# One square root fewer in the softmax reciprocal of an attention and expert-layer kernel

## The reference

```
h = layernorm(x)
q, k, v = split(h @ Wqkv.T)            # 16 heads of 64 features
lam = sigmoid(relu(log(t+1) @ Wl1.T) @ Wl2.T)   # one number per head and position
# attention inside 8 chunks of 256 positions
s = (q_chunk . k_chunk) / 8 * lam[key]
x = x + (softmax(s) @ v_chunk) @ Wout.T + bout
h = layernorm(x)
# 8 experts of width 1408, the two best per position, weighted by the softmax of the gate
# and a shared expert of width 2816, weighted by a sigmoid
x = x + sum_e w_e * down_e(silu(gate_e(h)) * up_e(h)) + sigmoid(h . seg) * shared(h)
```

## Time and profile before

| | |
|---|---|
| median of 3 runs | 3646.75 us (3646.26 to 3648.06) |
| the profiled execution | 3649.09 us, its slowest core's span 3647.6 us |
| spans of the 8 cores in it | 3639.4 to 3647.6 us, granted clock 0.894 to 0.897 |
| TensorE busy | 2927.1 us, 80% |
| VectorE busy | 1252.2 us, 34% |
| ScalarE busy | 906.0 us, 25% |

### The profile page before, as it was taken

The page is one execution under the profiler, slowest core; times in us unless marked ns, Lnnn a source line. Parts: engine busy times, 40 slices in busy tenths (PEclk is TensorE's granted clock), DMA queues, the critical chain, the costliest instruction groups (busy, mean ns, idle before and its releaser), DMA issues.

```text
span 3647.6 us, 38537 instructions; the slowest of 8 cores (3639.4 to 3647.6 us)
## 1 busy us (share of the span) xinstructions
PE 2927.1 (80%) x13760; PEld 1369.7 (38%) x13988; DVE 1252.2 (34%) x2411; ACT 906.0 (25%) x1560; POOL 58.0 (2%) x70
## 2 busy tenths in 40 slices
PE   0446545545645599999999999999999999999998
PEld 0223313313313244444444444444444444444443
DVE  0323323322322333333333333333333333334333
ACT  0275465465466211111111111111111111110110
POOL 0100000000000000000000000000000000000000
PEclk9966667757757699999999999999999999999999
DMA  8100000000000413203232032212320223203203
GB/s 163 23 1 1 1 1 1 1 1 1 1 1 1 69 27 52 44 3 50 44 52 39 6 52 44 37 23 37 53 44 9 44 44 52 44 1 53 44 1 93
DMA packets 14029, 114.31 MB, mean 31 GB/s; under 512 B 1931, under 2 KB 2060, under 8 KB 8212
## 3 DMA queue, kind: packets, MB, share of 16 engines
q0 software_dynamic: 6832, 94.95, 15.7%
q1 hardware_dynamic: 7012, 16.89, 1.8%
HBM read 198.39 MB, written 8.39 MB: 57 GB/s over the span
## 4 chain that ended last, share of the span: by engine, by line
PE 74%; ACT 11%; DVE 6%; issue 5%; SPq 2%; ACTq 1%; DVEq 0%; DMA 0%; POOL 0%; POOLq 0%
PE pb L182 73%; ACT arena L191 6%; ACT L191 5%; DVE arena L203 3%; SPq L237 2%; ACTq L199 1%; DVE arena L208 1%; DVE lnb L203 1%; DVE arena L218 1%; DVE arena L222 1%; PE pb L186 0%; DVE arena L213 0%; ACT arena L195 0%; DMA bl2s<-bl2c 0%; DVEq L178 0%
## 5 line engine op out<-in xcount | busy, mean ns | idle before, releaser
L182 PE MATMUL pb<-lnb,arena 128*128 128x512 bf16 (+1 forms) x7924 | 1645.7, 366 | 12.9 <-DVE lnb L203 5.1
L182 PEld LDWEIGHTS pb<-lnb,arena 128*128 128x128 bf16 x8064 | 788.3, 98 | 856.8 <-issue 14.6
L182 PE MATMUL pb<-arena 128*128 128x512 bf16 (+2 forms) x4472 | 973.1, 372 | 65.0 <-DVE arena L203 49.0
L191 ACT ACTIVATE arena<-pb 128x512 bf16<-128x512 f32 (+1 forms) x512 | 290.4, 567 | 2084.9 <-PE pb L182 2084.8
L203 DVE TENSOR_TENSOR arena<-pb,arena 128x512 bf16<-128x512 f32 (+1 forms) x568 | 358.4, 631 | 1152.5 <-PE pb L182 1145.3
L182 PEld LDWEIGHTS pb<-arena 128*128 128x128 bf16 (+1 forms) x4544 | 436.0, 102 | 562.3 <-issue 146.3
L203 DVE TENSOR_TENSOR res<-pb,res 128x512 f32<-128x512 f32 x640 | 442.8, 692 | 327.7 <-PE pb L182 323.2
L182 PE MATMUL pb<-arena,onesr 1*64 1x256 bf16 (+1 forms) x132 | 28.0, 403 | 259.3 <-ACT arena L191 259.1
L182 PE MATMUL pb<-arena,onesf_sb 128*128 128x256 bf16 (+1 forms) x432 | 120.7, 392 | 132.0 <-ACT arena L191 99.2
L191 ACT ACTIVATE arena<-arena 1x512 f32<-1x512 f32 (+6 forms) x385 | 195.0, 511 | 94.6 <-DVE arena L208 75.7
L203 DVE TENSOR_TENSOR arena<-arena 128x512 bf16<-128x512 bf16 (+3 forms) x496 | 196.0, 409 | 21.0 <-ACT arena L191 17.8
(11 more groups left out here) (46 smaller groups left out, 574.5 us busy)
## 6 DMA issues: line engine op xcount, KB each, us to landing
arena<-ffnw POOLq DMA_DIRECT2D x10, 3072.0 KB, 22.9
arena<-ffnw POOLq DMA_DIRECT2D x10, 2560.0 KB, 19.7
arena<-ffnw POOLq DMA_DIRECT2D x10, 1536.0 KB, 31.9
arena<-ffnw POOLq DMA_DIRECT2D x10, 1280.0 KB, 26.9
res<-xt SPq DMA_DIRECT2D x2, 4096.0 KB, 72.0
arena<-atnw POOLq DMA_DIRECT2D x4, 2048.0 KB, 31.8
out<-res SPq DMA_DIRECT2D x4, 2048.0 KB, 10.8
idn<-idn SPq DMA_DIRECT2D x1, 64.0 KB
```

What stands on the lines that cost most here:

```text
L182: Eng.matmul(o, l, r, start=st, stop=sp, skip_group_check=True))
L191: Eng.activation(o, i, f, bias=b, scale=s))
```

## The change

The second root and the DRAIN behind it are taken out, and the factor of the exponential goes from -4 to -2. Before, exp(-4 * ln(s^(1/4))) = 1/s; after, exp(-2 * ln(s^(1/2))) = 1/s.

```diff
@@ -716,11 +716,9 @@
         tok_s1 = act(RR, PB[bs0][0:1, 0:512], AF.Sqrt, bias=EPSR)
         bfree[bs0] = tok_s1
         wait("scalar", tok_s1)
-        act(RR, RR, AF.Sqrt, inc=False)
-        sdrain()
         act(RR, RR, AF.Ln, inc=False)
         sdrain()
-        rtok2[pp] = act(RRB, RR, AF.Exp, scale=-4.0)
+        rtok2[pp] = act(RRB, RR, AF.Exp, scale=-2.0)
```

## The result

| | before | after |
|---|---|---|
| median of the comparable executions | 3647.66 us (7) | 3602.49 us (6) |
| median of all | 3647.95 us (10) | 3602.95 us (9) |
| profiled execution | 3649.09 us | 3602.29 us |
| its spans, fastest and slowest core | 3639.4, 3647.6 us | 3594.8, 3600.7 us |

The ratio is 0.9878, with a 95% interval of 0.9866 to 0.9890: 45.2 us less by the medians.

The account below looks back on a forecast made before the run. The prediction took a closed turn of ScalarE and TensorE in the attention pairs as the bound. 3649.1 less 64 x 0.68 = 43.5 gives 3605.6, and 2.3 less for the median gives 3603.2 us, range 3597 to 3611.

Parts of the forecast that it names:

- The closed turn: Attention pairs: ScalarE and the matmuls take turns in a closed chain of 7.97 us, expected to become 7.29 us.
- The sum: Whole kernel: 0.68 us saved in each of 64 pairs, 43.5 us in all, giving 3603.2 us.
- All 64 pairs: Attention: every pair passes its saving on; rival with only 56 pairs counting, 38.1 us saved, 3608.7 us, 3 in 100.
- The slack read from the earlier trace: VectorE's layernorms beside the pairs: 2.07 us spare at a first pair, 1.35 and 1.53 at the tightest place, against 0.68.
- The load in its new place: Logarithm's table load, behind the first root's wait: starts at 605.60 instead of 606.28, saving 0.68 us a pair.
- Neither bound: Logarithm's load: earliest start 605.52, saving 48.6 us; settling behind the root until 606.16, saving 7.7 us, rival 3 in 100.
- this case: Uncovered skill-page drain behind the first root: load at 606.90, no gain, 3647 us, 1 in 100.
- The clock: Attention pairs: rival that TensorE's shorter idle time raises the clock, 12 us more gained, 3591 us, 4 in 100.
- the 5 allowed: Whole span: 5 us either way for changed points at which the granted clock rises.
- The slower rival: Chunks' dense stretches: the clock rises later, a quarter running cold loses 58 us, ending at 3661 us, 1 in 100.

## Why the prediction was right

- *The closed turn.* Right: turn 7.27 us after, 8.66 with a root more, 4.03 without any. Each instruction in the turn counted with its length and its gap.
- *The sum.* 0.68 us a pair was forecast, 0.70 came, since the load starts 0.75 us behind the start of the first root and not 0.77. 64 pairs make it 44.8 us, not 43.5. The measured medians stand 45.2 us apart. The median after is 3602.49 us against 3603.2 forecast; that it lies so near is in part luck, as the kernel before took 0.9 us more here than the 3646.75 that the forecast went from, and the gain was 1.7 us larger.
- *All 64 pairs.* Right: all turns shrank, those beside a layernorm too (14.50 to 13.80), and half the pairs gave half. The slack read from the earlier trace rows held. Its place was right: when 3.2 us more went, the layernorm of the earlier trace rows did become late.
- *The load in its new place.* The one cost that the trace didn't show came out 0.02 us from the value taken, the row of an ordinary wait. Neither bound was reached. The Trainium skill's "ScalarE: Activation LUTs", section "What ACT_TABLE_LOAD costs", has a drain of about 1.38 us beside each load. That doesn't hold here: 0.07 us stands between the root's end and the load. The price that the prediction gave this case, no change, was also mis-worked: a load at 606.90 in place of 606.28 would have made each pair 0.62 us longer, 40 us in all.
- *The clock.* It didn't rise in the pairs (0.50 over 582.53 to 647.53 us), and ScalarE's wait for the sums stayed at 0.81. What the two profiled executions differ by outside the pairs is 2.6 us, most of it ahead of the first pair, inside the 5 allowed. Even raised by added matmuls the clock gave 0.2 us to some turns, as priced, and 1.4 us between the medians, which is no more than groups differ by. That the shorter pause could have raised it was a possibility of the argument, not one that a run has shown.
- *The slower rival.* No sign: from the last pair of a chunk to the first of the next it is 488.9 us in all before and 483.4 after, 4.9 of the 5.5 being the seven last pairs' own; single ones of the seven moved by up to 1.6 us either way. Its price was a little low, since the two matmul times of the earlier trace rows make a wholly cold dense stretch 32 us longer, not 29; nothing hangs on that.

What the prediction didn't look for is that the larger cost stood next to the one removed: two loads of 1.28 us a pair, there only because of the first root. They come to 2 x 1.28 x 64 = 164 us, and with the root itself 200 us were measured.

## What to carry to other kernels

Before costing an instruction on a lightly loaded engine, follow the chain through one turn of the loop: if it closes on itself, each instruction in it costs its length times the turns, and the mean share says nothing. Then look at what the instruction brings with it, here a pair of table loads for one root that a scale factor can replace. And when a turn is opened by another order, count what the order adds where the loop starts, and list every resource that the moved instruction frees: the bank behind it closed another loop, which set the pace once the turn was short. What helped a long turn by 25 us cost a short one 40.

## What was unexpected

A higher granted clock bought almost nothing in the pairs: the mean over attention went from 0.71 to 0.77 and the medians lie 1.4 us apart. A DRAIN behind a met wait costs 0.04 us, and the exponential's bias from a tile 0.09 us on 0.63, both small, but they stand in the turn (7.27 to 7.31, and 4.03 to 4.12): 3 and 5 us over 64 pairs by the turns. The medians, 3.0 and 4.4 us apart, are of this size, but the kernels compared are of different groups. The scale of the logarithm cost nothing, 0.68 us with and without it.
